# Segment max: the one-hot of the segments' ends compared in bf16 with tile pairs innermost, and widened to fp32 on ScalarE

## The chip, the cores and the metric

The kernel runs on one core of a Trainium2 chip. The metric is the device time of one execution in microseconds (us); the time before is the median of three runs.

## The reference

A graph network of four layers over 3125 nodes and 100000 edges, sorted by destination. The change touches the second layer, whose attention needs, for each destination node, the maximum over its incoming edges of 256 logits:

```python
w_a = (efeat @ W_attn + b_attn).reshape(E, in_f, -1)
h_src = feat[src][:, :, None]
e2 = w_a * h_src
seg_max = jax.ops.segment_max(e2, dst, num_segments=N)
ex = jnp.exp(e2 - seg_max[dst])
denom = jax.ops.segment_sum(ex, dst, num_segments=N)
attn = ex / denom[dst]
ft = jax.ops.segment_sum(e1 * attn, dst, num_segments=N)
```

## The kernel before, in words

The edges lie in 832 tiles of 128 slots, in the order of their destinations; unused slots lie between blocks of nodes and at the end. Each stage of the kernel is a block in which every engine runs a queue of its own, ordered by semaphores. `segment_max` is one such stage: it takes the tiles in 208 batches of four (`HB = 4`, 512 slots), and everything before and after it waits at its borders.

For batch n, in the words of the code:

- POOL gathers the rows of the source nodes, one indirect DMA for a tile, into `ring`, which holds four batches (`DEEP = 4`); it may overwrite a batch once ScalarE has copied its features to `held`.
- PE turns the gathered rows (`src_ps`, L1429), ScalarE copies them (`src_t`, L1399) and copies the features to `held` (L1400), PE multiplies them out to 256 rows (`wide`, L1438) and makes the logits' other factor from the edges' features (`net`, L1443); ScalarE copies `wide` to `src_w` (L1405).
- DVE multiplies the two factors (`logit`, L1378) and runs a maximum along the slots, restarted at each segment by `far` (two scans, L1383). At the last slot of a segment the running maximum is the segment's. Then DVE makes the one-hot `hot` [128 slots, 4 tiles, 128 nodes] in fp32 (L1271): 1 where the slot is the end of a segment and the node is its own, from the field `LOE` of the slot.
- PE turns the running maxima (`back`, eight transposes in two PSUM tiles, L1456), ScalarE copies the two tiles (`run_e`, L1414), and PE multiplies `hot` by them (`best`, fp32, L1464). DVE subtracts `best` from the rows of `top` (`keep`, L1371).

The order in each queue is written out by hand. PE's is: src_ps, wide and net of batch n+1; then back and best of batch n. ScalarE's: src_t, held and src_w of batch n+1; then the two run_e of batch n. DVE's: logit, scans and hot of batch n; then keep of batch n-1.

Of the kernel before, what the change touches and what calls it, by code (L numbers as in the profile page):

```python
# [5 lines left out]
ALU = mybir.AluOpType  # L6
# [4 lines left out]
BF16 = mybir.dt.bfloat16  # L11
FP16 = mybir.dt.float16

P = 128
# [9 lines left out]
NT = -(-2 * ((E + NB * (2 * P - 1)) // (2 * P)) // (2 * TB)) * 2 * TB  # L24
# [7 lines left out]
WGT, SRC, TIX, LO, SRCC, KEY, LOE, NF = range(8)  # L32
# [24 lines left out]
def makers(nc, ctx, stage):  # L57

    def sb(name, shape, dt=F32):
        return ctx.enter_context(nc.sbuf_tensor(f"{stage}_{name}", shape, dt))  # L60

    def ps(name, shape, dt=F32):
        return ctx.enter_context(nc.psum_tensor(f"{stage}_{name}", shape, dt))

    def sem(name):
        made = nc.alloc_semaphore(f"{stage}_{name}")
        ctx.callback(PAST.append, made)
        return made

    return sb, ps, sem  # L70
# [738 lines left out]
def slot_field(m, t0, n, k):  # L809

    return m.fields[:, bass.ds(t0, n), k]


def blocks_of(nc, m, engine, pair, n):

    _, values = nc.values_load_multi_w_load_instructions(m.pair[0:1, bass.ds(pair, n)], engines=[engine], min_val=0, max_val=NB - 1,
                                                         skip_runtime_bounds_check_because=COUNTED)
    return values
# [412 lines left out]
HB = 4  # L1231
# [4 lines left out]
def batches(eng, total, first, last, body):  # L1236

    assert (total - first - last) % 2 == 0 and first % 2 == 1
    for n in range(first):
        body(n // 2, n % 2)  # L1240
    with eng.Fori(0, (total - first - last) // 2) as i:
        body(i + first // 2, 1)
        body(i + first // 2 + 1, 0)
    for n in range(total - last, total):
        body(n // 2, n % 2)


def fours(eng, total, body):

    for j in range(4):  # L1250
        body(0, j)
    with eng.Fori(0, total - 2) as i:
        for j in range(4):
            body(i + 1, j)
    for j in range(4):
        body(total - 1, j)


def inside(n, total=HT):

    return not isinstance(n, int) or 0 <= n < total


def wait(eng, sem, value):

    if not isinstance(value, int) or value > 0:
        eng.wait_ge(sem, value)


def one_hot(nc, m, field, n, out):  # L1270
    return nc.vector.tensor_tensor(out, slot_field(m, n * HB, HB, field)[:, :, None].to_broadcast([P, HB, P]),  # L1271
                                   m.iota_row[:, None, :].to_broadcast([P, HB, P]), ALU.is_equal)
# [47 lines left out]
def segment_max(nc, m):  # L1320

    DEEP = 4
    with ExitStack() as ctx:
        sb, ps, sem = makers(nc, ctx, "mx")
        idx, ring = sb("idx", [P, NT], I32), sb("ring", [P, DEEP, HB, W40])
        src_t, src_w = sb("src_t", [3 * D, 2, 512], BF16), sb("src_w", [P, 2, 512])
        feat, far, hot = sb("feat", [KP, 2, 512], BF16), sb("far", [P, 2, 512]), sb("hot", [P, 2, HB, P])
        logit, run, run_e = sb("logit", [P, 2, 512]), sb("run", [P, 2, 2, 512]), sb("run_e", [P, 2, HB, 256])
        src_ps, wide, net = ps("src_ps", [3 * D, 512], BF16), ps("wide", [P, 2, 512]), ps("net", [P, 2, 512])
        back, best = [ps("back0", [P, 2, 256]), ps("back1", [P, 2, 256])], ps("best", [P, 2, 256])  # L1330
        gathered, loaded = [sem(f"gathered{k}") for k in range(DEEP)], [sem("loaded0"), sem("loaded1")]
        names = ("idx_s", "src_s", "src_t_s", "wide_s", "src_w_s", "net_s", "logit_s", "run_s", "back_s", "run_e_s", "hot_s",
                 "best_s", "kept", "cleared", "held")
        (idx_s, src_s, src_t_s, wide_s, src_w_s, net_s, logit_s, run_s, back_s, run_e_s, hot_s, best_s, kept, cleared,
         held) = map(sem, names)
        block = ctx.enter_context(nc.Block())
        ring_bf = ring[:, :, :, :].bitcast(BF16)

        @block.sync
        def _(sp):  # L1340
            far_rows = m.far_row.rearrange("(c n) -> c n", n=512)
            feats = m.feat_t.rearrange("k (c n) -> k c n", n=512)

            def load(q, h):
                n = 2 * q + h
                wait(sp, run_s, n - 1)
                sp.dma_start(far[:, h], far_rows[bass.ds(n, 1)].to_broadcast([P, 512])).then_inc(loaded[h], 16)
                sp.dma_start(feat[:, h], feats[:, bass.ds(n, 1), :].rearrange("k o n -> k (o n)")).then_inc(loaded[h], 16)

            batches(sp, HT, 3, 1, load)  # L1350
# [11 lines left out]

        @block.vector
        def _(dve):
            def keep(n):
                blocks = blocks_of(nc, m, mybir.EngineType.DVE, 2 * n, 2)
                dve.wait_ge(best_s, n + 1)
                for k in range(2):
                    row = m.top[:, bass.ds(blocks[k], 1), :].rearrange("q o c -> q (o c)")
                    wait(dve, kept, 2 * n + k)  # L1370
                    nc.vector.tensor_tensor(row, row, best[:, k, :], ALU.subtract).then_inc(kept, 1)  # L1371

            def turn(q, h):
                n = 2 * q + h
                dve.wait_ge(net_s, n + 1)
                dve.wait_ge(src_w_s, n + 1)
                wait(dve, run_s, n)
                nc.vector.tensor_tensor(logit[:, :, :], net[:, :, :], src_w[:, :, :], ALU.mult).then_inc(logit_s, 1)  # L1378
                dve.wait_ge(loaded[h], (q + 1) * 32)
                dve.wait_ge(logit_s, n + 1)  # L1380
                for c in range(2):
                    before = run[:, 1 - h, c, 511:512] if inside(n - 1) else 0.0
                    last = nc.vector.tensor_tensor_scan(run[:, h, c, :], far[:, h, :], logit[:, c, :], before, ALU.add, ALU.max)  # L1383
                last.then_inc(run_s, 1)
                one_hot(nc, m, LOE, n, hot[:, h]).then_inc(hot_s, 1)
                if inside(n - 1):
                    keep(n - 1)

            nc.vector.tensor_copy(idx[:, :], m.fields[:, :, SRC]).then_inc(idx_s, 1)
            nc.vector.memset(m.top[:, :, :], 0.0).then_inc(cleared, 1)  # L1390
            dve.wait_ge(cleared, 1)
            batches(dve, HT, 3, 3, turn)
            keep(HT - 1)

        @block.scalar
        def _(act):
            def sources(n, k):
                act.wait_ge(src_s, n + 1)
                nc.scalar.copy(src_t[:, k % 2], src_ps[:, :]).then_inc(src_t_s, 1)  # L1399
                nc.scalar.copy(m.held[:, bass.ds(n * HB, HB), :], ring[:, k, :, 0:D]).then_inc(held, 1)  # L1400

            def widened(n):
                act.wait_ge(wide_s, n + 1)
                wait(act, logit_s, n)
                nc.scalar.copy(src_w[:, :, :], wide[:, :, :]).then_inc(src_w_s, 1)  # L1405

            def turn(q, j):
                n, h = 4 * q + j, j % 2
                if inside(n + 1):
                    sources(n + 1, (j + 1) % 4)  # L1410
                    widened(n + 1)
                for k in range(2):
                    act.wait_ge(back_s, 2 * n + k + 1)
                    nc.scalar.copy(run_e[:, h, 2 * k:2 * k + 2, :], back[k][:, :, :]).then_inc(run_e_s, 1)  # L1414

            sources(0, 0)
            widened(0)
            fours(act, HT // 4, turn)
# [774 lines left out]
def build(nc, a, out):  # L2193
# [17 lines left out]
    with ExitStack() as ctx:  # L2211
# [44 lines left out]
        with ExitStack() as scope:  # L2256
            rb = on(scope)
            m.top3, m.held = rb("top3", [P, NB, 3, 256], BF16), rb("held", [P, NT, D])
            normalise(nc, m, "n1")
            attention_rows(nc, m)  # L2260
            with ExitStack() as tops:
                m.top = on(tops)("top", [P, NB, 256])
                segment_max(nc, m)
                split_top(nc, m)
            m.acc = rb("acc", [P, NB, 512])
            soft_sums(nc, m)
            attend(nc, m)
# [52 lines left out]
```

## Time and profile before

| | us |
|---|---|
| median of 3 runs (lowest to highest) | 8238.34 (8218.16 to 8241.7) |
| the profiled execution, its own time | 8244.08 |
| span of its trace | 8242.4 |
| segment max in the trace, first `logit` to last `keep` | 2822.37 to about 3970.5 |

Times in the trace count from the start of the span. A stretch is read by what ends the idle time ahead of an instruction on its engine: the "releaser". Instructions of one engine that follow without a pause may overlap by a tenth of a microsecond in the records, since the next starts before the last has written its end.

### The profile page before, as it was taken

Reading aid. Unit: us, or ns where it says so; the run is one execution under the profiler, and the core shown is the slowest. Engines: PE = TensorE matmul, PEld = TensorE weight load, DVE = VectorE, ACT = ScalarE, POOL = GpSimd, SP = SyncE. Lnnn points to the kernel's source line nnn. Section 1 sums busy time; section 2 is a strip of 40 time slices with the busy share of each in tenths; the row PEclk is TensorE's granted clock in tenths of the full one; section 3 lists DMA queues with packets and bytes.
Section 4 is the critical chain, followed back from the end, with each engine's and each line's share of the span. In section 5 each row is a group of like instructions: output and inputs, shape, how many; then the busy total and the mean of one; then the engine's idle time right before and its main releaser. Section 6 shows DMA issues by size and latency. Waiting matters only on the chain. (4 is left out here: it accounts for less than half of the span.)

```text
span 8242.4 us, 120531 instructions
## 1 busy us (share of the span) xinstructions
PE 5734.8 (70%) x33629; PEld 3891.4 (47%) x33630; DVE 5955.1 (72%) x11485; ACT 1609.0 (20%) x2672; POOL 4496.5 (55%) x4143
## 2 busy tenths in 40 slices
PE   3433333256444588887699999455479699999999
PEld 2333333146444455555455555144334366666555
DVE  5766555275333499998899999799600388888898
ACT  0010111101000255554122222044000022222000
POOL 0488888487777577777377777200000277777000
PEclk9999999855555699999899999699889655555899
DMA  2122222332111333334211111022263411112000
GB/s 99 41 60 57 56 55 58 77 83 53 37 37 36 49 84 85 83 85 79 42 44 43 44 43 44 15 109 110 80 264 136 151 32 32 32 32 32 1 0 1
DMA packets 486789, 514.88 MB, mean 62 GB/s; under 512 B 258365, under 2 KB 388805, under 8 KB 476106
## 3 DMA queue, kind: packets, MB, share of 16 engines
q1 hardware_dynamic: 343198, 446.64, 17.5%
q0 software_dynamic: 132160, 43.97, 6.7%
q10 hardware_dynamic: 11232, 21.73, 0.9%
q8 instruction: 111, 1.82, 0.1%
q14 instruction: 88, 0.72, 0.0%
HBM read 415.02 MB, written 95.99 MB: 62 GB/s over the span
## 5 line engine op out<-in xcount | busy, mean ns | idle before, releaser
L1284 POOL DMA_INDIRECT sh_ring<-node,sh_idx x832 | 858.6, 1032 | 1488.2 <-DVE sh_idx L1921 1229.4
L424 POOL DMA_INDIRECT slots<-rank_staged,rank_row_i x800 | 998.7, 1248 | 265.5 <-issue 260.0
L1533 POOL DMA_INDIRECT slots<-sm_rec,sm_row x832 | 900.0, 1082 | 388.0 <-issue 215.2
L1360 POOL DMA_INDIRECT mx_ring<-node,mx_idx x832 | 857.8, 1031 | 322.3 <-issue 248.5
L935 POOL DMA_INDIRECT mid_ring<-typed,mid_idx x832 | 875.8, 1053 | 259.2 <-issue 253.4
L404 PE MATMUL rank_found<-rank_next_sb,rank_hot_hi_t 25*125 25x128 f32 x1600 | 374.3, 422 | 764.0 <-ACT rank_next_sb L386 748.5
L1643 PE MATMUL sm_sums<-sm_both,sm_hot 128*128 128x512 f32 x1664 | 786.8, 595 | 0.4 <-DVE sm_both L1564 0.2
L404 PEld LDWEIGHTS rank_found<-rank_next_sb,rank_hot_hi_t 25*125 25x125 f32 x1600 | 347.4, 323 | 789.8 <-issue 734.9
L1140 PE MATMUL mid_sums<-mid_ring,mid_hot_d 128*128 128x17 f32 x1664 | 391.7, 375 | 459.3 <-DMA mid_ring<-typed,mid_idx 446.9
L1140 PEld LDWEIGHTS mid_sums<-mid_ring,mid_hot_d 128*128 128x128 f32 x1664 | 383.3, 312 | 476.0 <-issue 476.0
L2161 PE MATMUL srl_sums<-srl_outer,srl_hot_lo 128*128 128x400 f32 x1664 | 561.9, 501 | 7.4 <-DVE srl_outer L2143 7.4
L1383 DVE TENSOR_TENSOR_SCAN mx_run<-mx_far,mx_run,mx_logit 128x512 f32<-128x512 f32 x414 | 509.1, 1272 | 21.5
L695 PE MATMUL adj_sums<-adj_heavy,adj_hot 128*128 128x128 bf16 x4224 | 322.7, 222 | 244.0 <-DVE adj_heavy L644 129.1
L1464 PE MATMUL mx_best<-mx_run_e,mx_hot 128*128 128x256 f32 x1664 | 418.8, 395 | 50.7 <-ACT mx_run_e L1414 50.3
L2161 PEld LDWEIGHTS srl_sums<-srl_outer,srl_hot_lo 128*128 128x128 f32 x1664 | 317.4, 191 | 252.8 <-DVE srl_outer L2143 9.1
L2061 PE MATMUL sh_hid_ps<-sh_ends_t,mlp 32*128 32x512 f32 x416 | 392.8, 1096 | 56.8 <-ACT sh_ends_t L2014 56.8
L1601 ACT ACTIVATE sm_both<-sm_net_a 128x512 f32<-128x512 f32 x416 | 248.6, 598 | 938.1 <-PE sm_net_a L1630 933.7
L695 PEld LDWEIGHTS adj_sums<-adj_heavy,adj_hot 128*128 128x128 bf16 x4224 | 245.0, 98 | 323.2 <-issue 275.5
L1053 DVE COPY mid_ring<-fields 128x8 f32<-128x8 f32 x104 | 18.8, 181 | 505.0 <-PE mid_sums L1142 505.0
L1643 PEld LDWEIGHTS sm_sums<-sm_both,sm_hot 128*128 128x128 f32 x1664 | 283.2, 190 | 209.8 <-issue 200.7
L1707 DVE TENSOR_TENSOR agg<-c_sums,dinv_row 128x3200 f32<-128x3200 f32 x4 | 14.0, 3492 | 501.8 <-PEq L1746 501.8
L2068 PE MATMUL sh_v_ps<-mlp,sh_hid 128*128 128x32 f32 x1664 | 374.5, 401 | 0.0
(404 smaller groups left out, 12727.3 us busy)
## 6 DMA issues: line engine op xcount, KB each, us to landing
strips<-near SPq DMA_DIRECT2D x76, 1600.0 KB, 14.4
mx_far<-far_row SPq DMA_DIRECT2D x208, 256.0 KB
rank_key_row<-key_rows SPq DMA_DIRECT2D x100, 488.3 KB
near<-adj_whole SPq DMA_DIRECT2D x175, 256.0 KB, 2.0
sm_low<-low_row SPq DMA_DIRECT2D x208, 128.0 KB
sh_low<-low_row SPq DMA_DIRECT2D x104, 256.0 KB, 3.3
feat_t<-mid_out ACTq DMA_DIRECT2D x104, 204.0 KB
mx_feat<-feat_t SPq DMA_DIRECT2D x208, 102.0 KB
```

The lines of the kernel that those rows point to most:

```text
L404: last = nc.tensor.matmul(found[h][:, j, :], hot_hi_t[:, h, j, :], next_sb[:, h, j * P:(j + 1) * P], start=True, stop=True, skip_group_che ...
L424: pool.indirect_dma_start(m.slots, bass.IndirectOffsetOnAxis(ap=row_i[:, h, j:j + 1], axis=0), staged[:, h, j, :], None).then_inc(sent[h], 16)
L695: last = nc.tensor.matmul(sums[:, bass.ds(at[j], P)], hot[:, h, j // 2, :, j % 2], heavy[:, h, k, j // 2, :, j % 2], start=False, stop=Tru ...
L935: pool.indirect_dma_start(ring[:, n % DEEP, j, 0:D], None, m.typed, bass.IndirectOffsetOnAxis(ap=idx[:, t:t + 1], axis=0)).then_inc(gather ...
L1140: nc.tensor.matmul(sums[:, bass.ds(blocks[j // 2] * K17, K17)], hot_d[:, h, j, :], ring[:, n % DEEP, j, 0:K17], start=False, stop=True, sk ...
L1284: pool.indirect_dma_start(ring[:, h, j, :], None, table, bass.IndirectOffsetOnAxis(ap=idx[:, h, j:j + 1], axis=0)).then_inc(part, 16)
L1360: pool.indirect_dma_start(ring[:, n % DEEP, j, :], None, m.node40, bass.IndirectOffsetOnAxis(ap=idx[:, t:t + 1], axis=0)).then_inc(gathere ...
L1383: last = nc.vector.tensor_tensor_scan(run[:, h, c, :], far[:, h, :], logit[:, c, :], before, ALU.add, ALU.max)
L1464: last = nc.tensor.matmul(best[:, k, :], hot[:, h, 2 * k + j, :], run_e[:, h, 2 * k + j, :], start=j == 0, stop=j == 1, skip_group_check=True)
L1533: pool.indirect_dma_start(m.slots2, bass.IndirectOffsetOnAxis(ap=row2[:, t:t + 1], axis=0), rec2[:, t, :], None).then_inc(ordered, 16)
L1643: last = nc.tensor.matmul(sums[r % 2][:, :], hot[:, h, 2 * (r % 2) + j, :], both[:, r % 2, j].rearrange("q a c -> q (a c)"), start=j == 0, ...
L2161: last = nc.tensor.matmul(sums[:, 0:NB * D], hot_lo[:, h, j, :], outer[:, h, j, :], start=False, stop=True, skip_group_check=True)
```

## The change

The one-hot is no longer made in fp32 by DVE. DVE keeps two new tables, made once at the stage's start: `loe16`, the ends' nodes of all slots in bf16, and `iota`, the numbers 0 to 127, each twice. For each batch it compares them into `hot16`, bf16, laid out with two tiles innermost: [2 pairs of tiles, 128 nodes, 2 tiles], so that the innermost step of every operand is one 16-bit element. ScalarE then copies `hot16` to `hot`, fp32 in the old layout (a cast that reads at a step of two elements), between its copy of `wide` for batch n+1 and its two copies of `back` for batch n. PE's matmuls are as they were. DVE now waits for the ScalarE copy of batch n-2 before it writes `hot16` of batch n again, and ScalarE waits for `hot16` of batch n and for `best` of batch n-2.

```diff
+        loe16, iota, hot16 = sb("loe16", [P, NT], BF16), sb("iota", [P, P, 2], BF16), sb("hot16", [P, 2, HB // 2, P, 2], BF16)
...
+            pairs = [P, HB // 2, P, 2]
...
                 last.then_inc(run_s, 1)
-                one_hot(nc, m, LOE, n, hot[:, h]).then_inc(hot_s, 1)
+                wait(dve, hot_s, n - 1)
+                nc.vector.tensor_tensor(hot16[:, h], loe16[:, bass.ds(n * HB, HB)].rearrange("q (a t) -> q a t", t=2)[:, :, None, :].to_broadcast(pairs),
+                                        iota[:, None, :, :].to_broadcast(pairs), ALU.is_equal).then_inc(hot16_s, 1)
...
             nc.vector.memset(m.top[:, :, :], 0.0).then_inc(cleared, 1)
-            dve.wait_ge(cleared, 1)
+            nc.vector.tensor_copy(loe16[:, :], m.fields[:, :, LOE]).then_inc(cleared, 1)
+            nc.vector.tensor_copy(iota[:, :, :], m.iota_row[:, :, None].to_broadcast([P, P, 2])).then_inc(cleared, 1)
+            dve.wait_ge(cleared, 3)
...
                     sources(n + 1, (j + 1) % 4)
                     widened(n + 1)
+                act.wait_ge(hot16_s, n + 1)
+                wait(act, best_s, n - 1)
+                nc.scalar.copy(hot[:, h].rearrange("q (a t) c -> q a t c", t=2), hot16[:, h].rearrange("q a c t -> q a t c")).then_inc(hot_s, 1)
                 for k in range(2):
                     act.wait_ge(back_s, 2 * n + k + 1)
                     nc.scalar.copy(run_e[:, h, 2 * k:2 * k + 2, :], back[k][:, :, :]).then_inc(run_e_s, 1)
```

On ScalarE, one turn of the stage's loop stands so before (`mx_` is the stage's prefix; ISA and REGISTER_ALU rows are waits and loop arithmetic):

```order
L1399 COPY mx_src_t<-mx_src_ps 48x512
L1400 ISA
L1400 COPY held<-mx_ring 128x64
L1405 COPY mx_src_w<-mx_wide 128x1024
L1413 ISA
L1414 COPY mx_run_e<-mx_back 128x512
L1413 REGISTER_ALU
L1414 COPY mx_run_e<-mx_back 128x512
```

And so in the changed kernel, where the lines have moved down by some:

```order
L1406 COPY mx_src_t<-mx_src_ps 48x512
L1407 ISA
L1407 COPY held<-mx_ring 128x64
L1412 COPY mx_src_w<-mx_wide 128x1024
L1267 REGISTER_ALU
L1421 CAST mx_hot<-mx_hot 128x512
L1423 ISA
L1424 COPY mx_run_e<-mx_back 128x512
L1423 REGISTER_ALU
L1424 COPY mx_run_e<-mx_back 128x512
```

One instruction has come in, the cast (`mx_hot` stands here for both `hot` and `hot16`), behind the copy of `wide` and ahead of the first copy of `back`. On DVE the stage begins so before:

```order
L1389 CAST mx_idx<-fields 128x832
L1390 MEMSET top 128x6400
L1378 TENSOR_TENSOR mx_logit<-mx_net,mx_src_w 128x1024
L1383 SCALAR_TENSOR_TENSOR mx_run<-mx_far,mx_logit 128x512 x2
L1271 TENSOR_TENSOR mx_hot<-fields,iota_row 128x512
```

And so in the changed kernel:

```order
L1394 CAST mx_idx<-fields 128x832
L1395 MEMSET top 128x6400
L1396 CAST mx_loe<-fields 128x832
L1397 CAST mx_iota<-iota_row 128x256
L1381 TENSOR_TENSOR mx_logit<-mx_net,mx_src_w 128x1024
L1386 SCALAR_TENSOR_TENSOR mx_run<-mx_far,mx_logit 128x512 x2
L1389 TENSOR_TENSOR mx_hot<-mx_loe,mx_iota 128x512
```

Two casts have come in ahead of the first `logit`, and the one-hot stands at its old place with its new operands; PE, POOL and SyncE have the same rows as before.

## Rows read from the trace of the kernel before

**Rows 1.** The page: its span, and the busy time of each engine.

```profile
span 8242.4 us, 120531 instructions
PE 5734.8 (70%) x33629; PEld 3891.4 (47%) x33630; DVE 5955.1 (72%) x11485; ACT 1609.0 (20%) x2672; POOL 4496.5 (55%) x4143
```

**Rows 2.** Windows: stretch, length, busy us of each engine, clock, DMA share, GB/s.

```profile
2850.00:3880.00 1030.00, 841.39 (x4626) 547.56 (x4625) 963.03 (x1157) 535.12 (x963) 794.62 (x773) 1.00 0.36 84
3880.00:3950.00 70.00, 40.69 (x185) 26.57 (x184) 38.46 (x48) 21.94 (x39) 33.99 (x33) 0.78 0.80 51
1000.00:1500.00 500.00, 188.06 (x960) 169.27 (x960) 297.41 (x997) 51.41 (x80) 402.77 (x320) 1.00 0.27 56
```

**Rows 3.** Timeline of DVE: `logit` of the first batch and of the 200th.

```profile
2822.37 1.23 DVE L1378 TENSOR_TENSOR mx_logit<-mx_net,mx_src_w 128x1024 f32<-128x1024 f32 x1 [3.43 <-ACT mx_src_w L1405]
...
3888.65 1.23 DVE L1378 TENSOR_TENSOR mx_logit<-mx_net,mx_src_w 128x1024 f32<-128x1024 f32 x1
```

**Rows 4.** Waits, 2850 to 3880 us: total, times, longest.

```profile
PE mx_wide L1438 <- ACT mx_src_t L1399: 128.9, 192, 0.7
ACT mx_src_w L1405 <- PE mx_wide L1438: 105.7, 193, 0.6
PE mx_best L1464 <- ACT mx_run_e L1414: 47.4, 193, 0.4
DVE mx_logit L1378 <- ACT mx_src_w L1405: 9.0, 31, 1.2
PE mx_src_ps L1429 <- DMA mx_ring<-node,mx_idx: 7.9, 28, 1.2
```

**Rows 5.** Timeline, one batch: start, us, engine, line, operation, count, idle before.

```profile
3407.70 1.99 PE L1464 MATMUL mx_best<-mx_run_e,mx_hot 128*128 128x256 f32 x8 [0.24 <-ACT mx_run_e L1414]
...
3409.62 0.40 PE L1429 MATMUL mx_src_ps<-ident_bf,mx_ring 128*48 128x128 bf16 x4
3410.06 0.58 ACT L1399 COPY mx_src_t<-mx_src_ps 48x512 bf16<-48x512 bf16 x1 [1.93 <-PE mx_src_ps L1429]
3410.55 0.24 ACT L1400 COPY held<-mx_ring 128x64 f32 x1
...
3410.70 0.60 PE L1438 MATMUL mx_wide<-mx_src_t,widen 48*128 48x512 bf16 x2 [0.67 <-ACT mx_src_t L1399]
...
3411.12 0.69 DVE L1271 TENSOR_TENSOR mx_hot<-fields,iota_row 128x512 f32<-128x512 f32 x1
...
3411.34 1.01 ACT L1405 COPY mx_src_w<-mx_wide 128x1024 f32<-128x1024 f32 x1 [0.55 <-PE mx_wide L1438]
...
3411.68 1.04 PE L1456 MATMUL mx_back<-ident,mx_run 128*128 128x128 f32 x8
...
3412.31 1.07 ACT L1414 COPY mx_run_e<-mx_back 128x512 f32<-128x512 f32 x2
...
3412.95 0.48 PE L1464 MATMUL mx_best<-mx_run_e,mx_hot 128*128 128x256 f32 x1 [0.24 <-ACT mx_run_e L1414]
```

**Rows 6.** The gathers, 2850 to 3880 us: ns min/median/max, first and last start.

```profile
L1360 POOL DMA_INDIRECT mx_ring<-node,mx_idx x773: 943/947/1722, 2849.5 to 3880.0; - x194
```

**Rows 7.** Groups by line and shape, DVE, whole span: busy us, mean ns of one.

```profile
L1371 DVE TENSOR_TENSOR top<-top,mx_best 128x256 f32 x416 | 172.4, 414 | 35.1 <-DVE top L1371 4.6 <-PE mx_best L1464 4.3
L1271 DVE TENSOR_TENSOR mx_hot<-fields,iota_row 128x512 f32<-128x512 f32 x208 | 143.4, 689 | 0.0
...
L640 DVE TENSOR_TENSOR adj_near<-adj_now,adj_iota 128x1024 bf16<-128x1024 bf16 x176 | 121.8, 692 | 6.0
```

**Rows 8.** Two ScalarE copies from SBUF to SBUF: ns min/median/max.

```profile
L388 ACT COPY rank_staged<-edges x100: 346/352/353, 277.2 to 1515.1; 125x192 f32 x100
L1400 ACT COPY held<-mx_ring x208: 242/243/245, 2820.0 to 3958.7; 128x64 f32 x100, 128x64 f32<-128x64 f32 x4
```

**Rows 9.** Timeline of PE in one batch in the stage's last part.

```profile
3913.88 1.91 PE L1456 MATMUL mx_back<-ident,mx_run 128*128 128x128 f32 x8
...
3915.62 3.38 PE L1464 MATMUL mx_best<-mx_run_e,mx_hot 128*128 128x256 f32 x8
```

More of the change, by code:

```diff
@@ L1332, in segment_max @@
         names = ("idx_s", "src_s", "src_t_s", "wide_s", "src_w_s", "net_s", "logit_s", "run_s", "back_s", "run_e_s", "hot_s",
-                 "best_s", "kept", "cleared", "held")
+                 "best_s", "kept", "cleared", "held", "hot16_s")
         (idx_s, src_s, src_t_s, wide_s, src_w_s, net_s, logit_s, run_s, back_s, run_e_s, hot_s, best_s, kept, cleared,
-         held) = map(sem, names)
+         held, hot16_s) = map(sem, names)
         block = ctx.enter_context(nc.Block())
```

## The prediction

> **What bounds the kernel now.** I read the page first, to place the stage: the span is 8242.4 us, DVE and PE are each busy about 70% of it and ScalarE 20% [rows 1]. Such shares say nothing about this change, since only one stage is touched, so I went to the windows of that stage. From 2850 to 3880 us DVE is busy 963 of 1030 us, PE 841, POOL 795, ScalarE 535 [rows 2]. DVE looks like the bound, and the change takes work from DVE and gives it to an engine that is half idle. The question is whether the order of events agrees.
>
> The pace: from the first to the 200th `logit` 199 batches pass in 1066.3 us, 5.36 us each [rows 3]. The remaining eight run through a stretch in which the DMA engines are 80% busy and PE only 41 of 70 us [rows 2]; there the gathers and loads set the pace.
>
> The waits show the loop that the batches turn in [rows 4]. PE's `wide` waits for ScalarE's `src_t` in 192 batches, ScalarE's `src_w` for `wide` in 193, PE's `best` for ScalarE's `run_e` in 193, all of about 193 batches in the stretch. DVE's `logit` waits for `src_w` in only 31. So two engines hand the work to and fro in every single batch, and DVE runs beside them, mostly just in time. One batch on the timeline gives the links [rows 5], start to start: `best` to `src_ps` 1.92 (PE works through eight matmuls), `src_ps` to `src_t` 0.44, `src_t` to `wide` 0.64, `wide` to `src_w` 0.64, `src_w` to `run_e` 0.97, `run_e` to the next `best` 0.64. Their sum is 5.25 us, with no slack in any link. The queue orders close this loop: `src_ps` stands behind `best` on PE, and `run_e` behind `src_w` on ScalarE.
>
> POOL is a second loop. Its 773 gathers start 1.335 us apart (1030.5 us over 772) [rows 6], so four take 5.34 us. That is 0.09 more than the PE-ScalarE loop and just about the measured pace. The 28 times that PE waited for a gather, 7.9 us in all [rows 4], are what is visible of it; the rest hides in a slightly late start of `src_ps`. So today POOL paces the stage at 5.34 to 5.36, the PE-ScalarE loop could do 5.25, and DVE fits under both.
>
> **The change part by part.**
>
> DVE, the one-hot: 0.69 us now [rows 7]. The new form, 512 elements from bf16 to bf16 with pairs innermost, has a sister: L640, 1024 elements in 0.692 us, where the fp32 form takes 0.689 for 512 [rows 7]. So an element costs half. An fp32 operation of 256 elements takes 0.41 (L1371) and should be the new price; the gain on DVE is 0.28 us a batch, and between nothing and 0.28 if the layout were read at the old rate. But neither the PE-ScalarE loop nor POOL waits for DVE here, so on the time this gain is worth 0. It only makes DVE wait longer for `src_w`.
>
> ScalarE, the cast: 128x512, SBUF to SBUF. The two nearest rows are 0.243 us for 64 elements and 0.352 for 192 [rows 8], 0.85 ns per element more, which gives 0.62 for 512. From below, the copies of 512 from PSUM take 0.59 each (two in 1.07, one starting before the other's end) [rows 5]. I take 0.62. When one follows another directly, the second starts about 0.1 before the end of the first: `held` at 3410.55 behind `src_t`, whose end is 3410.64 [rows 5]. So the pitch is 0.52.
>
> Where it falls decides. Ahead of `src_t` ScalarE is idle for 1.93 us in a batch and ahead of `src_w` for 0.55 [rows 5]; there the cast would be free. But it stands behind `src_w` and ahead of `run_e`, in the one link of the loop that has ScalarE work back to back. It can't start earlier, since ScalarE takes its queue in order. Its input is there in time: the one-hot started at 3411.12, before `src_w` began at 3411.34 [rows 5], and after the change is shorter still; so no wait for DVE. The other new waits (DVE for the cast of n-2, ScalarE for `best` of n-2) are for things done a batch earlier.
>
> The new link from `src_w` to `run_e`: `src_w` takes 1.01, less 0.1 overlap puts the cast's start at +0.91; +0.52 puts `run_e` at +1.43, where it was +0.97. That is 0.46 more, and the loop becomes 5.25 + 0.46 = 5.71 us. `back` is ready by then (it now begins 0.63 before `run_e`, and is tied to `net` on PE, not to the cast). What is queued behind the cast is `run_e`, for it waits `best`, and for `best` waits `src_ps` of the next batch: the whole loop. At 5.71 POOL's 5.34 is no longer the pace; POOL will wait for `held`. So of the 0.46 the first 0.11 only fills what POOL cost already: 5.71 against 5.36 is 0.35 us a batch.
>
> The Trainium skill has a formula for the cast (ScalarE: Activation LUTs, What ACT_TABLE_LOAD costs): 186 ns plus 0.833 ns per element with immediate scale, back-to-back ones overlapping by 93 ns. An estimate from that page is 613 ns and a pitch of 0.52, the same link to the hundredth; no row here shows a cast that reads at a step of two. The same page's rules for kernel authors lean against the move as such: they send simple elementwise arithmetic to VectorE rather than ScalarE, for its speed per element. Carried over to this copy, the widening would sit on DVE, where another pass over 512 elements would undo the gain; the rule does not ask where in a loop the work falls, which is what decides here.
>
> The start: two more casts on DVE, 832 and 256 elements. At the one-hot's rate they are about 1.1 and 0.4 us, together 1.5. They fall in the 3.43 us that DVE waits before the first `logit` [rows 3], so 0; without that cover 1.5 us once.
>
> The sum: 198 batches by 0.35 are 69 us. The last eight add at most 0.46 each and nothing where DMA holds them; I count 1 us. 8244.08 + 70 = 8314 for an execution like the profiled one; that one stood 5.7 above the median of the runs shown, so the median forecast is 8308.
>
> Bounds. Low: a cast of 0.59 with 0.1 overlap, a link 0.43 longer, 5.68, 198 by 0.32 are 63 us: 8302. High: no overlap on either side of the cast, 1.01 + 0.62 = 1.63 against 0.97, 0.66 longer, 5.91, 198 by 0.55 and 2 are 111 us: 8349.
>
> **The rivals.**
>
> DVE is the bound after all, and the cast hides. DVE is busy 93.5% of the stretch and is seen to wait for ScalarE only 9 us [rows 2, 4]; its work is 963 us over some 193 batches, 5.0 each, besides what it loses between instructions. If the loop through ScalarE had slack behind it, the stage would win what DVE sheds, 0.28 by 198, or 55 us: 8183. The point from which this decides is a slack of 0.46 in `run_e` to `best`. Against it: `best` waits for `run_e` in all 193 batches, and POOL at 5.34 would stop the gain at once unless gathers sped up too.
> The Trainium skill gives a way for that (GPSIMD Engine Reference, Specifications): GpSimd's SBUF interfaces are shared with VectorE, in contention when a DVE instruction has two SBUF inputs, as this one-hot has before and after. The gather closest to a one-hot on the profile does not support it: the median gather, 947 ns, is 4 ns above the shortest [rows 6]. As a mechanism of this kernel: were the gathers' pitch to fall and the cast to hide, the loop's 5.25 would be the limit, 0.11 by 198, 22 us less: 8216. I give 0.04 to a gain over 0.3%.
>
> No change. The cast hides, POOL keeps its 5.34: 8238. It needs a loop link that absorbs 0.37 us, which rows 5 don't have. 0.05.
>
> The clock falls. In the last part of the stage PE, waiting for data, ran its eight `best` matmuls in 3.38 us against 1.99, and `back` in 1.91 against 1.04 [rows 5, 9]; the window's granted clock was 0.78 [rows 2]. The change lowers PE's share from 82% to about 77%. At 1.2 GHz throughout, `best` alone adds 1.39 a batch and `wide`, 0.60 now, about 0.4 by the same ratio: 1.8 by 198, some 355 us on the forecast, 8660. Against it: a stretch with PE busy 38% had the full 2.4 GHz [rows 2], and the longest idle time of PE in a batch stays at about 0.7. 0.04.
>
> The 16-bit form does not run at double rate: DVE's 5.0 us of work a batch stay as they are, below 5.71, and the time is that of my forecast. It is inside it.
>
> **How the numbers follow.** The forecast mechanism has 0.87. With the clock's 0.04 slower is 0.91, no change 0.05, faster 0.04. The 0.3% is 25 us, about what a measurement of this kernel can tell from no change. Since the runs before scatter over 24 us, the range goes from 8302 less most of that, 8280, to the high bound, 8350, and leaves out the three rivals.
>
> **What would show it.** Right: `src_w` to `run_e` at 1.4 us start to start; a cast of about 0.6 in every batch; `best` still waiting for `run_e` every time, with PE idle 0.7 instead of 0.24 before it; batches 5.7 apart; POOL waiting for `held` in most batches; DVE's one-hot at 0.41 and DVE waiting for `src_w` in nearly all; the other stages the same. Wrong: a cast much longer than 0.62 because of its step-two read, a cast that waits for `hot16`, a pace that stays at 5.36, or a granted clock below 1.00 in the stage.

## The result, and the profile after

The changed kernel takes 8302.76 us (median of 6 runs, 8299.06 to 8310.25) against 8229.99 us for the kernel before on the same occasions (6 runs, 8218.16 to 8241.7): ratio 1.0092, 95% interval 1.008 to 1.0103. It is 73 us slower (66 to 85 by the interval); 70 were forecast, and 8302.76 lies in the range.

The page of the changed kernel, span and busy time of each engine, beside [rows 1]:

```profile
span 8297.3 us, 121048 instructions
PE 5725.8 (69%) x33629; PEld 3889.1 (47%) x33630; DVE 5917.4 (71%) x11487; ACT 1704.1 (21%) x2880; POOL 4554.6 (55%) x4143
```

DVE's busy time is 38 us shorter and ScalarE's 95 longer. The one-hots alone shed 56 us (208 at 0.69, now at 0.42) and the two new casts add 1; where the other 17 lie was not looked into. The two traces differ by 55 us in span and not by 73, because the stages ahead of this one took 14 us less in the second: the first `logit` starts at 2822.37 before and at 2807.9 after. The stage itself is best taken alone. From its first `logit` to its last it takes 1138.2 us before and 1209.5 after, 71 more. The timeline of DVE, first and 200th `logit` (the line is L1381 now), answers to [rows 3]:

```profile
L1381 DVE TENSOR_TENSOR mx_logit<-mx_net,mx_src_w x208: 1224/1225/1226, 2807.9 to 4017.4; 128x1024 f32<-128x1024 f32 x104
```

```profile
3944.67 1.23 DVE L1381 TENSOR_TENSOR mx_logit<-mx_net,mx_src_w 128x1024 f32<-128x1024 f32 x1 [0.79 <-ACT mx_src_w L1412]
```

So 199 batches in 1136.8 us, 5.71 each, against 5.36; the last eight take 73 us, as before (72). The window of the stage's body (columns as in [rows 2]) shows PE at 76%, with the full clock:

```profile
2850.00:3940.00 1090.00, 828.85 (x4582) 540.72 (x4581) 911.25 (x1146) 616.96 (x1146) 857.17 (x765) 1.00 0.35 79
```

One batch on the timeline, to lay beside [rows 5]:

```profile
3408.49 1.99 PE L1474 MATMUL mx_best<-mx_run_e,mx_hot 128*128 128x256 f32 x8 [0.69 <-ACT mx_run_e L1424]
3408.95 2.46 DVE L1386 TENSOR_TENSOR_SCAN mx_run<-mx_far,mx_run,mx_logit 128x512 f32<-128x512 f32 x2
3409.22 1.76 POOL L1361 DMA_INDIRECT mx_ring<-node,mx_idx  x1 [0.30 <-issue]
...
3410.41 0.40 PE L1439 MATMUL mx_src_ps<-ident_bf,mx_ring 128*48 128x128 bf16 x4
3410.86 0.58 ACT L1406 COPY mx_src_t<-mx_src_ps 48x512 bf16<-48x512 bf16 x1 [1.93 <-PE mx_src_ps L1439]
3411.29 0.94 POOL L1361 DMA_INDIRECT mx_ring<-node,mx_idx  x1 [0.30 <-issue]
3411.33 0.42 DVE L1389 TENSOR_TENSOR mx_hot<-mx_loe,mx_iota 128x512 bf16<-128x512 bf16 x1
...
3412.13 1.01 ACT L1412 COPY mx_src_w<-mx_wide 128x1024 f32<-128x1024 f32 x1 [0.55 <-PE mx_wide L1448]
...
3413.04 0.62 ACT L1421 CAST mx_hot<-mx_hot 128x512 f32<-128x512 bf16 x1
3413.23 1.23 DVE L1381 TENSOR_TENSOR mx_logit<-mx_net,mx_src_w 128x1024 f32<-128x1024 f32 x1 [0.59 <-ACT mx_src_w L1412]
3413.55 1.08 ACT L1424 COPY mx_run_e<-mx_back 128x512 f32<-128x512 f32 x2
...
3414.20 1.99 PE L1474 MATMUL mx_best<-mx_run_e,mx_hot 128*128 128x256 f32 x8 [0.69 <-ACT mx_run_e L1424]
```

The cast takes 0.62 and has a pitch of 0.51 (3413.04 to 3413.55). The link from `src_w` to `run_e` is 1.42 (3412.13 to 3413.55) where it was 0.97, and `best` comes 5.71 after `best`. PE now stands idle 0.69 ahead of `best` in place of 0.24. The one-hot takes 0.42 in place of 0.69, and DVE uses the time to wait for `src_w`. The waits of the body, beside [rows 4]:

```profile
PE mx_best L1474 <- ACT mx_run_e L1424: 132.6, 191, 0.7
DVE mx_logit L1381 <- ACT mx_src_w L1412: 131.7, 191, 1.2
...
PE mx_src_ps L1439 <- DMA mx_ring<-node,mx_idx: 0.4, 1, 0.4
```

Two things there were not foreseen. POOL is nowhere seen waiting for `held`, though by the prediction's 5.34 it has 0.4 us a batch too much; and one gather of four lasts 1.6 to 1.8 us. The experiments turn on these.

### The profile page after: what moved, and what is told of

It reads as the page before. It is cut to its first block and busy times, and to the rows that moved or that the text cites. A ratio compares the mean times of both kernels' runs of the same rounds, so it can differ in the third digit from the quotient of the medians.

```text
span 8297.3 us, 121048 instructions
## 1 busy us (share of the span) xinstructions
PE 5725.8 (69%) x33629; PEld 3889.1 (47%) x33630; DVE 5917.4 (71%) x11487; ACT 1704.1 (21%) x2880; POOL 4554.6 (55%) x4143
## 5 line engine op out<-in xcount | busy, mean ns | idle before, releaser
L424 POOL DMA_INDIRECT slots<-rank_staged,rank_row_i x800 | 977.0, 1221 | 264.9 <-issue 255.5
L1361 POOL DMA_INDIRECT mx_ring<-node,mx_idx x832 | 935.4, 1124 | 320.1 <-issue 252.9
L1474 PEld LDWEIGHTS mx_best<-mx_run_e,mx_hot 128*128 128x128 f32 x1664 | 302.4, 192 | 223.5 <-ACT mx_run_e L1424 183.2
L1381 DVE TENSOR_TENSOR mx_logit<-mx_net,mx_src_w 128x1024 f32<-128x1024 f32 x208 | 254.7, 1225 | 178.4 <-ACT mx_src_w L1412 151.3
```

Source lines behind the costliest of these rows:

```text
L424: pool.indirect_dma_start(m.slots, bass.IndirectOffsetOnAxis(ap=row_i[:, h, j:j + 1], axis=0), staged[:, h, j, :], None).then_inc(sent[h], 16)
L1361: pool.indirect_dma_start(ring[:, n % DEEP, j, :], None, m.node40, bass.IndirectOffsetOnAxis(ap=idx[:, t:t + 1], axis=0)).then_inc(gathere ...
L1474: last = nc.tensor.matmul(best[:, k, :], hot[:, h, 2 * k + j, :], run_e[:, h, 2 * k + j, :], start=j == 0, stop=j == 1, skip_group_check=True)
```

## The experiments

The kernels are told apart by the stage's own numbers, since whole executions of one kernel scatter: those of the kernel before spread over 24 to 53 us (8202.18 to 8255.01 beside e1 to e4). At least 26 us lie in the stages ahead: in eight traces from chips on which the kernel before takes about 8225, the first `logit` starts anywhere from 2797 to 2823 us. "Body" is the mean distance of the logits from the 21st to the 181st batch, "stage" is first to last `logit`, all read from the traces' timelines:

| | body, us a batch | stage, us | last eight, us |
|---|---|---|---|
| before | 5.35 | 1138.2 | 71.9 |
| before, second trace (e11) | 5.37 | 1141.3 | 68.2 |
| changed | 5.71 | 1209.5 | 72.7 |
| e1, DVE half alone | 5.25 | 1118.4 | 66.8 |
| e2, ScalarE half alone | 5.72 | 1207.7 | 68.7 |
| e3, cast early | 5.31 | 1127.3 | 67.1 |
| e4, three gathers | 5.31 | 1102.7 | 44.8 |
| e12, loop cut | 5.36 | 1142.9 | 70.7 |

**e1, only the DVE half.**

```diff
-                wait(dve, hot_s, n - 1)
                 nc.vector.tensor_tensor(hot16[:, h], loe16[:, bass.ds(n * HB, HB)].rearrange("q (a t) -> q a t", t=2)[:, :, None, :].to_broadcast(pairs),
-                                        iota[:, None, :, :].to_broadcast(pairs), ALU.is_equal).then_inc(hot16_s, 1)
+                                        iota[:, None, :, :].to_broadcast(pairs), ALU.is_equal).then_inc(hot_s, 1)
...
-            dve.wait_ge(cleared, 3)
+            nc.vector.memset(hot[:, :, :, :], 0.0).then_inc(cleared, 1)
+            dve.wait_ge(cleared, 4)
...
-                act.wait_ge(hot16_s, n + 1)
-                wait(act, best_s, n - 1)
-                nc.scalar.copy(hot[:, h].rearrange("q (a t) c -> q a t c", t=2), hot16[:, h].rearrange("q a c t -> q a t c")).then_inc(hot_s, 1)
```

> Only the DVE half of the change: the one-hot is made in bf16 with pairs innermost, the cast is left out, and PE reads a constant tile of zeros in place of the one-hot (so the segment maxima are left out of the output). Three theories of what paced the kernel before at 5.36 us a batch. (1) DVE's own queue paced it: its logits start 5.21 and 5.43 us apart in turn, 5.32 on average, with the PE-ScalarE loop at 5.25 right behind. Then the one-hot's 0.27 us come off DVE and the loop stops the gain: batches 5.25 apart, about 22 us less than before, near 8210. (2) POOL paced it at 5.34, as predicted: nothing changes, batches 5.34 apart, and before's time within 5 us. (3) DVE alone and no loop near it: batches 5.05 apart, about 60 us less.

Measured: 8221.58 us against 8222.71, ratio 1.0001 (0.9988 to 1.0014). In the trace the body is 5.25 and the stage 20 us shorter than before's. Waits of its body, 2850 to 3830 us:

```profile
POOL mx_ring L1361 <- ACT held L1407: 54.2, 178, 0.3
...
DVE mx_logit L1381 <- ACT mx_src_w L1412: 36.0, 96, 1.9
PE mx_src_ps L1436 <- DMA mx_ring<-node,mx_idx: 3.0, 5, 1.5
```

The pace is the PE-ScalarE loop's 5.25 to the hundredth, which falsifies POOL's 5.34: the same 832 gathers went through at 5.25. POOL's waits for `held` are no slack: they last 0.3 us, like the pause that stands ahead of every gather. So theory 1 holds for the body. The 20 us don't show in the medians, whose interval allows 10 at most, and theory 1 expected 22 less there; one trace is one draw from the scatter above, so whether the whole keeps any of the gain stays open.

**e2, only the ScalarE half.**

```diff
-                one_hot(nc, m, LOE, n, hot[:, h]).then_inc(hot_s, 1)
+                wait(dve, hot_s, n - 1)
+                one_hot(nc, m, LOE, n, made[:, h]).then_inc(made_s, 1)
...
+                act.wait_ge(made_s, n + 1)
+                wait(act, best_s, n - 1)
+                nc.scalar.copy(hot[:, h], made[:, h]).then_inc(hot_s, 1)
```

> Only the ScalarE half: DVE makes the one-hot in fp32 as before, into a buffer of its own, and ScalarE copies it fp32 to fp32 at the place where the changed kernel has its cast. If the link from src_w to run_e decides and DVE's gain is worth nothing there, batches are 5.71 us apart as in the changed kernel and the time is within 10 us of it, some 72 above before. If the cheaper one-hot gave something back, this kernel is slower than the changed one by up to 0.27 us a batch, 55 us. A cast that costs more than a plain copy for its step-two read would show as a shorter link than 1.43 us.

Measured: 8300.78 us, ratio to before 1.0099 (1.0082 to 1.0116), where the changed kernel has 1.0092 (1.008 to 1.0103). ScalarE on its timeline:

```profile
3407.62 1.02 ACT L1407 COPY mx_src_w<-mx_wide 128x1024 f32<-128x1024 f32 x1 [0.55 <-PE mx_wide L1443]
3408.53 0.62 ACT L1416 COPY mx_hot<-mx_made 128x512 f32<-128x512 f32 x1
3409.05 1.08 ACT L1419 COPY mx_run_e<-mx_back 128x512 f32<-128x512 f32 x2
```

The plain fp32 copy costs 0.62 like the cast from bf16 at a step of two, and the link is 1.43. The whole loss comes from the ScalarE half, and in its company the cheaper one-hot is worth nothing (stage 1207.7 and 1209.5).

**e3, the change with the cast early.**

```diff
+            def ends16(n, h):
+                nc.vector.tensor_tensor(hot16[:, h], loe16[:, bass.ds(n * HB, HB)].rearrange("q (a t) -> q a t", t=2)[:, :, None, :].to_broadcast(pairs),
+                                        iota[:, None, :, :].to_broadcast(pairs), ALU.is_equal).then_inc(hot16_s, 1)
...
-                wait(dve, hot_s, n - 1)
-                nc.vector.tensor_tensor(hot16[:, h], loe16[:, bass.ds(n * HB, HB)].rearrange("q (a t) -> q a t", t=2)[:, :, None, :].to_broadcast(pairs),
-                                        iota[:, None, :, :].to_broadcast(pairs), ALU.is_equal).then_inc(hot16_s, 1)
+                if inside(n + 1):
+                    wait(dve, hot_s, n)
+                    ends16(n + 1, 1 - h)
...
+            ends16(0, 0)
...
-                if inside(n + 1):
-                    sources(n + 1, (j + 1) % 4)
-                    widened(n + 1)
                 act.wait_ge(hot16_s, n + 1)
                 wait(act, best_s, n - 1)
                 nc.scalar.copy(hot[:, h].rearrange("q (a t) c -> q a t c", t=2), hot16[:, h].rearrange("q a c t -> q a t c")).then_inc(hot_s, 1)
+                if inside(n + 1):
+                    sources(n + 1, (j + 1) % 4)
+                    widened(n + 1)
```

> The whole change with the cast moved: DVE makes the bf16 one-hot of batch n+1 in turn n, and ScalarE casts it first in its turn, ahead of src_t, where it was idle 1.93 us. If the place of the cast is what costs, the PE-ScalarE loop is back at 5.25 and the link from src_w to run_e at 0.97. With theory 1 (DVE paced before) batches come 5.25 apart, some 22 us under before. With theory 2 (POOL paces at 5.34) they come 5.34 apart and the time is before's within 5 us. If the cast costs wherever it stands (a shared resource), they stay near 5.7.

Measured: 8218.89 us, ratio 0.9999 (0.9988 to 1.001); body 5.31, stage 11 us under before's, which the medians don't show. The cast stands in idle time, and the link is 0.98, against 0.97 before:

```profile
3405.41 0.63 ACT L1423 CAST mx_hot<-mx_hot 128x512 f32<-128x512 bf16 x1
...
3407.46 0.58 ACT L1411 COPY mx_src_t<-mx_src_ps 48x512 bf16<-48x512 bf16 x1 [1.41 <-PE mx_src_ps L1444]
...
3408.73 1.01 ACT L1417 COPY mx_src_w<-mx_wide 128x1024 f32<-128x1024 f32 x1 [0.55 <-PE mx_wide L1453]
...
3409.71 1.07 ACT L1429 COPY mx_run_e<-mx_back 128x512 f32<-128x512 f32 x2
```

The same work on the same engines costs 73 us in one place and nothing that the medians can tell in another. The body lies between the theories' 5.25 and 5.34. DVE, with the cheaper one-hot, waits for `src_w` in 111 of 184 batches, so it is not the bound here; `best` mostly follows `best` at the loop's 5.25, and PE was 12 times late for a gather, 5.2 us in all.

**e4, three gathers of four.** Against the kernel before; what the fourth gather would have brought is read from the first or the third.

```diff
-                for j in range(HB):
+                for j in range(HB - 1):
...
-                nc.scalar.copy(m.held[:, bass.ds(n * HB, HB), :], ring[:, k, :, 0:D]).then_inc(held, 1)
+                nc.scalar.copy(m.held[:, bass.ds(n * HB, HB), :], ring[:, k, 0:1, 0:D].to_broadcast([P, HB, D])).then_inc(held, 1)
...
-                pe.wait_ge(gathered[k], (q + 1) * 16 * HB)
+                pe.wait_ge(gathered[k], (q + 1) * 16 * (HB - 1))
...
-                    last = nc.tensor.transpose(src_ps[:, j * P:(j + 1) * P], ring_bf[:, k, j, 2 * D:2 * W40], m.ident_bf[:, :])
+                    last = nc.tensor.transpose(src_ps[:, j * P:(j + 1) * P], ring_bf[:, k, min(j, HB - 2), 2 * D:2 * W40], m.ident_bf[:, :])
```

> The kernel before with three gathers a batch in place of four; the fourth tile takes the rows of the third (so a quarter of the sources' rows are left out of the output). It takes a quarter of POOL's work away and leaves the others as they are. Theory 2 (POOL paces at 5.34): the pace falls to the loop's 5.25, 20 us less, and POOL waits for held. Theory 1 (DVE paces at 5.32): the pace stays at 5.32 to 5.34 in the body of the stage; only the last part, where gathers land late, may get shorter by up to 20 us.

Measured: 8189.32 us, ratio 0.996 (0.9945 to 0.9974), 33 less. The body is 5.31; 27 of the stage's 35 us come from the last eight batches, 45 us in place of 72, where at most 20 were expected. Waits of the body, 2850 to 3830 us:

```profile
POOL mx_ring L1360 <- ACT held L1400: 330.2, 185, 2.0
```

With POOL out of the way (it waits 1.8 us a batch) the pace does not reach 5.25, and DVE's `logit` does not appear in the list of waits at all: DVE goes at 5.31 by its own queue. That is what paced the kernel before. The 0.04 above it go with late gathers: before, PE was 28 times late for one, 7.9 us over 192 batches, and DVE waited 9.0 us for `src_w` [rows 4]; here neither wait is left.

**e5, the cast twice.**

```diff
+                nc.scalar.copy(spare[:, HB * h:HB * h + HB].rearrange("q (a t) c -> q a t c", t=2), hot16[:, h].rearrange("q a c t -> q a t c"))
                 nc.scalar.copy(hot[:, h].rearrange("q (a t) c -> q a t c", t=2), hot16[:, h].rearrange("q a c t -> q a t c")).then_inc(hot_s, 1)
```

> The changed kernel with the cast issued twice in a row, the first into a scratch tile. The theory that the cast's whole pitch lies on the loop of PE and ScalarE says that the second costs its pitch of 0.52 us in every batch: 6.23 us a batch in place of 5.71, 208 by 0.52 or 104 to 108 us more, about 8408. If ScalarE or DVE had slack there, or if PE's clock reacts to the longer idle time, it is less or more than that.

Measured: 9124.52 us, where the kernel before took 9113.71 on that chip: ratio 1.0014 (1.0002 to 1.0026). e5 to e8 ran on one chip, e9 and e10 on another, on which the kernel before takes 9114 and 9121 us in place of 8225. In the traces from them the batches are uneven, 6.1 to 6.9 us in e5 and 5 to 10 or more in the others, so whole times say little about this stage. The changed kernel itself was not run there. An even piece of e5's timeline gives its loop:

```profile
3404.13 1.99 PE L1476 MATMUL mx_best<-mx_run_e,mx_hot 128*128 128x256 f32 x8 [1.21 <-ACT mx_run_e L1426]
...
3410.36 1.99 PE L1476 MATMUL mx_best<-mx_run_e,mx_hot 128*128 128x256 f32 x8 [1.21 <-ACT mx_run_e L1426]
```

6.23 us from `best` to `best`, with 1.21 idle ahead of it, as the theory has it (5.71 + 0.52); over the whole body the batches are 6.40 apart. The forecast of the whole time, about 8408, missed: it was made for a chip of the other kind. With two casts the kernel is only 11 us over before here, where one cast cost 73 on the other chips, so the price of the cast's place is shown for those alone.

**e8, the scans read one SBUF tensor.**

```diff
-                nc.vector.tensor_tensor(logit[:, :, :], net[:, :, :], src_w[:, :, :], ALU.mult)
+                nc.vector.tensor_tensor(net[:, :, :], net[:, :, :], src_w[:, :, :], ALU.mult)
...
-                    last = nc.vector.tensor_tensor_scan(run[:, h, c, :], far[:, h, :], logit[:, c, :], before, ALU.add, ALU.max)
+                    last = nc.vector.tensor_tensor_scan(run[:, h, c, :], far[:, h, :], net[:, c, :], before, ALU.add, ALU.max)
...
-                wait(pe, logit_s, n)
+                wait(pe, run_s, n)
```

> The kernel before with the logit multiplied in place in PSUM, so that each scan reads one tensor from SBUF and one from PSUM in place of two from SBUF; PE's net of batch n+1 waits for the scans of batch n. In all traces so far one gather of four is stretched (1.14 to 1.9 us against 0.95) and the next one starts just where the second scan ends. If scans with two SBUF tensors hold the gathers up, here no gather is stretched, all are at 0.94 to 0.95, POOL gets four batches ahead and waits for held. If the stretch has another cause it stays. The pace: DVE's 5.31 plus what a PSUM read adds to two scans, up to 0.15, so up to 25 us slower.

Measured: 9156.06 us against 9113.71, ratio 1.0047 (1.0033 to 1.0062), on the first of the two slower chips; up to 25 us more were expected, and it is 42. The timeline of DVE and POOL:

```profile
3399.84 0.67 DVE L1271 TENSOR_TENSOR mx_hot<-fields,iota_row 128x512 f32<-128x512 f32 x1
3399.90 1.42 POOL L1360 DMA_INDIRECT mx_ring<-node,mx_idx  x1 [0.56 <-ACT held L1400]
...
3402.64 2.45 DVE L1383 TENSOR_TENSOR_SCAN mx_run<-mx_far,mx_run,mx_net 128x512 f32<-128x512 f32 x2
3402.88 0.95 POOL L1360 DMA_INDIRECT mx_ring<-node,mx_idx  x1 [0.30 <-issue]
3404.13 0.94 POOL L1360 DMA_INDIRECT mx_ring<-node,mx_idx  x1 [0.30 <-issue]
```

Gathers that start inside the two scans take 0.95 here. From 3200 to 3800 us there are 76 that start between 0.1 and 1.1 us into the scans, and none is stretched. Before, in the same stretch of time, all 112 that started 0.43 to 0.91 us into the scans were, to 1.13 to 1.61; in the changed kernel all 105 that started 0.26 to 0.49 into them were, to 1.55 to 1.77; and in e7, from the same chip as e8, 51 of the 52 that started 0.4 to 1.1 into them. So a scan with two SBUF tensors holds a gather up. The expected "none at all" was too strong: all 39 gathers that started just after the one-hot had begun took 1.3 to 1.4. The one-hot still reads two SBUF tensors, and it holds a gather too; in the kernel before, gathers start just ahead of the one-hot and none inside it, so none is held there.

This also explains how POOL can move at the pace of the batches and never wait. In the traces of before, changed, e1 and e3 the gather that follows a held one starts 0.12 us ahead of the end of the pair of scans, whatever the pace. Three gathers at 1.25 bring the fourth into the next pair of scans, and the first scan of the pair holds it: in the bodies of these traces every gather held there ends 0.75 to 0.77 us after the end of that first scan, wherever it began. The second scan, which begins during the same gather, adds nothing. By estimate from these numbers the held gather starts 6.08 us less the pace into the scans: 0.7 at 5.35, 0.4 at 5.71, 0.8 at 5.25, and the traces have 0.43 to 0.91, 0.26 to 0.49 and 0.72 to 0.94. So there POOL took the pace of DVE's scans and did not set it.

**e6, e9 and e12, the loop cut.** The same kernel three times, e3's with `src_ps` of batch n+2 ahead of `best` of batch n on PE, and `src_t` and `held` behind `run_e` on ScalarE:

```diff
                 if inside(n + 1):
-                    sources(q + (i + 1) // 4, (i + 1) % 4)
                     logits(q + (i + 1) // 4, (i + 1) % 4)
...
+                if inside(n + 2):
+                    sources(q + (i + 2) // 4, (i + 2) % 4)
                 pe.wait_ge(hot_s, n + 1)
```

> The change with the cast early, and the loop cut: PE makes src_ps of batch n+2 ahead of best of batch n, and ScalarE copies it behind run_e of batch n, so that best no longer stands in the loop. Then DVE is the next bound: its own chain is 5.31 us in the run with three gathers, less 0.27 for the cheaper one-hot, 5.04; four gathers take 5.0 plus what the scans stretch them by. With DVE as the bound batches come 5.04 to 5.1 apart, 45 to 60 us under before. If the gathers' stretches (0.2 to 0.4 in a batch now) add to their 5.0, POOL paces at 5.2 to 5.3 and the gain is 10 to 25 us.

> The kernel of e6 once more (bf16 one-hot, early cast, src_ps of batch n+2 ahead of best of batch n), since in that call before itself took 9114 us and every kernel had batches of 5 to 10 us in no order. On a chip on which before takes about 8225: with DVE as the next bound batches are 5.04 to 5.1 us apart, 45 to 60 us under before; with POOL as the bound (four gathers of 1.25 plus the scans' stretches) 5.2 to 5.3, 10 to 25 us under.

> The kernel of e6 for the third time, beside before on the same chip. If before takes about 8225 there: DVE or POOL is the next bound, batches 5.04 to 5.3 us apart, 10 to 60 us under before. If before takes 9110: 70 us slower than before again, and the two traces show in which waits the batches of this kernel lose more than before's.

Measured: ratio 1.0087 (1.0071 to 1.0102) and 1.008 (1.0066 to 1.0093) on the two slower chips, and on a chip like the first, 8246.48 us against 8230.06, ratio 1.0022 (1.0012 to 1.0031). It was meant to beat both kernels and loses to before. The waits of e12's body, 2850 to 3830 us, show where:

```profile
PE mx_back L1472 <- DVE mx_run L1390: 81.3, 157, 0.8
...
PE mx_src_ps L1446 <- DMA mx_ring<-node,mx_idx: 45.2, 20, 2.9
...
POOL mx_ring L1361 <- ACT held L1412: 4.3, 14, 0.3
```

Batches that nothing disturbs come 4.93 and 5.13 apart, so DVE's queue is at its 5.04. But POOL, which hardly waits, starts only 746 gathers in 1000 us, 5.36 a batch: 5.0 for four and the rest in stretched ones, since at this pace some gathers fall behind the start of the one-hot:

```profile
3502.25 0.39 DVE L1369 TENSOR_TENSOR mx_hot<-mx_loe,mx_iota 128x512 bf16<-128x512 bf16 x1
3502.33 1.14 POOL L1361 DMA_INDIRECT mx_ring<-node,mx_idx  x1 [0.31 <-issue]
```

Twenty times PE stops for a gather, 2.3 us on average, and after such a stop its clock is lower for a while:

```profile
2994.12 0.38 PE L1446 MATMUL mx_src_ps<-ident_bf,mx_ring 128*48 128x128 bf16 x4 [2.74 <-DMA mx_ring<-node,mx_idx]
2994.44 3.63 PE L1482 MATMUL mx_best<-mx_run_e,mx_hot 128*128 128x256 f32 x8
```

In 18 batches of the body the eight `best` matmuls take 2.6 to 3.8 us in place of 1.99. The granted clock is 0.72 from 2992 to 2998 us and 0.96 in the body. All this points to POOL as the bound here; but no run took gathers away from this kernel, so that is argued and not shown.

**e7 and e10, the loop cut alone,** fp32 one-hot and no cast, the same PE and ScalarE orders as above.

> The kernel before with only the loop cut (src_ps of batch n+2 ahead of best of batch n), the one-hot in fp32 on DVE as before and no cast. If DVE paced before, at 5.31, nothing is to be had: batches 5.31 to 5.34 apart, the time of before within 8 us. If the PE-ScalarE loop or POOL paced it through a late src_ps, the pace falls below 5.31. Beside the run above it shows what the 16-bit one-hot is worth once the loop is out of the way: the difference of the two should be up to 0.27 us a batch, 55 us.

> The kernel of e7 once more (fp32 one-hot on DVE, no cast, src_ps of batch n+2 ahead of best of batch n), for the same reason. If DVE's own chain paced the kernel before, at 5.31 us, cutting the loop gives nothing: batches 5.31 to 5.34 apart and before's time within 8 us, and the run above is 40 to 55 us under this one. If DVE was not the bound, this kernel gains as well.

Measured: ratios 1.0022 (1.0009 to 1.0035) and 1.0017 (1.0007 to 1.0027), both on the slower chips: 22 and 18 us over before, where at most 8 were expected, and 51 to 55 us less than e6 and e9 beside them. That is no gain, but with bodies of 6.54 and 6.44 us a batch these runs don't test what paces the kernel at 5.35. The comparison that was wanted, what the 16-bit one-hot is worth with the loop cut, came out the other way round there, and why was not settled on those uneven traces.

**e11, before once more.**

> The kernel before, unchanged, for a second trace of it. The trace of before at hand took 8244 us, while 20 executions on a later chip had a median of 8223. On a chip of that kind the body of the stage should again run at 5.34 us a batch with one gather of four stretched by a scan, and the 20 us should lie in the stages ahead of it, or else the body of the stage varies too, which would lessen what the runs without the cast (5.25 and 5.29 a batch) gained. On a chip on which before takes 9110, its batches should be as irregular as those of the other kernels there, about 6.3 to 6.6 us on average.

Measured: 8229.61 us against 8230.06, ratio 0.9999 (0.9989 to 1.0008). Its stage starts uneven (5.5 us a batch for the first 60) and goes on at 5.33; the stage takes 1141.3, so the 21 us by which its trace's span is shorter lie in the stages ahead.

## Why the prediction was right, and which step was wrong

The loop and the place of the cast: right, and shown on the chips on which the kernel before takes about 8225. The forecast link was 1.43 and is 1.42; the loop 5.71 and is 5.71; 198 batches by 0.35 and 1 us for the rest are 70, and the stage grew by 71. e2 shows that the ScalarE half alone makes the loss, e3 that the place does. In e5, in an even piece on a slower chip, a second cast adds its pitch of 0.52. The whole time grew by 73 and its interval is some 20 us wide, so that 70 and 73 lie so close is in part luck; the stage's 71 is the better check.

The prices: the one-hot 0.41, measured 0.42; the cast 0.62, measured 0.62. Reading at a step of two cost nothing (e2). The two casts at the start took 0.77 and 0.28, under the 1.1 and 0.4 of the estimate, and hid behind the wait for the first `logit`.

PE's clock: 1.00 in the body, as before, with PE at 76%.

What paced the kernel before: wrong. "So today POOL paces the stage at 5.34 to 5.36" took the gathers' mean distance for POOL's own speed. The gathers went at 5.25 in e1 as well, and with a quarter of them gone (e4) the pace was still 5.31, with DVE never waiting for `src_w`. DVE's own queue was the bound, 5.31, with the PE-ScalarE loop 0.06 under it and late gathers adding 0.04. The 5.34 held a quarter of gathers that the scans had stretched, so it was DVE's pace read off POOL. The sum was untouched, since it set the new loop against the measured 5.36 and not against a cause.

From this the expectation "POOL will wait for `held`" failed too: in the changed kernel POOL is held up inside one gather of four, by the scans, 1.55 to 1.77 us against 0.94, so the trace shows no wait.

The rival "DVE is the bound after all" was half right. DVE was the bound; but the loop behind it was near, so that even with the cast out of the way the body gains 0.04 to 0.10 a batch (e3, e1) and not 0.28.

The dismissal of the shared interface was a misreading. The text held that the median gather is 4 ns above the shortest [rows 6]; the maximum in that same row is 1722 ns, and it is a quarter of the gathers that is stretched, which a median hides. The rule that was cited there (the Trainium skill, GPSIMD Engine Reference, Specifications: contention when a DVE instruction has two SBUF inputs) agrees with e8 for the scans, and for the one-hot by the 39 gathers that began inside it there. In the kernel before it is the scans that do it, since no gather begins inside the one-hot that was looked at.

## What to carry to other kernels

Before work is moved to an idle engine, find the loop that the batches turn in and the link in which that engine already works back to back: there a copy with a pitch of 0.52 us made the loop 0.46 longer, though the engine was 52% busy, and ahead of `src_t` in the same queue, with its input made a batch earlier, it cost nothing that could be measured.

An engine that never seems to wait and moves at the common pace is not thereby the bound; take a part of its work away and see whether the pace changes. And when bounds stand 0.05 us apart, as DVE's queue and the PE-ScalarE loop did here, removing one buys only the distance to the next.

## What was not expected of the hardware

A tensor-tensor scan of DVE with both tensors in SBUF holds up a gather that GpSimd starts 0.26 to 0.91 us after the first of two scans began (217 of 217 in the traces of before and changed, 3200 to 3800 us); the gather lasts 1.13 to 1.77 us in place of 0.95 and ends 0.75 to 0.76 us after that one scan, though the next scan has begun by then. With one of the two tensors in PSUM it does not (none of 76 in e8). A one-hot with two SBUF inputs does it too (39 of 39 in e8), and the gather ends 0.81 to 0.83 us after it. Gathers that were already under way as a scan began were not held: none of those just ahead of a pair, and in e12 none of the 58 that started 1.1 to 1.25 us into it, about as its second scan begins.

Two of the chips used took 9114 to 9121 us for the kernel that takes 8223 to 8230 on the others, with the same duration of DVE's and ScalarE's instructions in this stage and with uneven gaps between them. Some gaps have no releaser in the profile: in e10's stage, 3200 to 4200 us, `best` stood idle 46 times so, up to 4.5 us; e12's body on the other chip has no such gap. The cause was not found.
